# A fused conditioned block with an LSTM: a later reciprocal, an attention product and injections at other steps, and a scan that adds first

## What is computed

```
# L0: attention over two keys (a learned no-op and the condition), 16 heads
w = softmax(q @ k);  x = x + (w @ v) @ W_proj + b_proj
# L1: one shared SwiGLU expert, 8 routed gelu experts, top 2 by a sigmoid router
s = sigmoid(x @ router_w.T + t_bias)
topk of s + router_bias;  denom = sum of the 2 chosen s
gates = s_sel / (denom + EPS)  (1/2 where denom <= EPS)
x = x + (shared + sum of gates * expert) / 3
# L2: x = x + u @ W_u + x @ W_e,   u = gelu(cond @ W_proj + b_proj)
# L3: an LSTM over the 1024 tokens, 256 wide
z = x_t @ Wx + b + h @ Wh;  i, f, o = sigmoid(z_i), sigmoid(z_f), sigmoid(z_o);  g = tanh(z_g)
c = f * c + i * g;  h = o * tanh(c);  y_t = x_t + h
```

## Time and profile before

| | before |
|---|---|
| median of 3 runs | 2413.18 us (2410.02 to 2414.47) |
| the profiled execution | 2409.16 us |
| its span, first to last instruction | 2407.4 us |
| granted TensorE clock, share of full speed | 0.996 |
| PE busy, PEld busy | 2051.9 us (85%), 1505.9 us (63%) |
| DVE, POOL, ACT busy | 1420.3 us (59%), 1169.1 us (49%), 876.7 us (36%) |

### The profile page before, as it was taken

How to read it: one execution, slowest core, us unless ns; L and a number is a source line. 1 busy time by engine, 2 the same in 40 slices (tenths; PEclk the granted TensorE clock), 3 DMA queues, 4 the chain that set the end, 5 groups by cost and what they waited for, 6 DMA issues and landing times.

```text
span 2407.4 us, 200920 instructions
## 1 busy us (share of the span) xinstructions
PE 2051.9 (85%) x86306; PEld 1505.9 (63%) x86306; DVE 1420.3 (59%) x7602; ACT 876.7 (36%) x4761; POOL 1169.1 (49%) x5082
## 2 busy tenths in 40 slices
PE   6888888888888888888888888888888888888888
PEld 4666666666666666666666666666666666666666
DVE  2565665566566556656655665665566566556655
ACT  1333333333333333333333333333333333333333
POOL 3445445444544554454455445445544544544454
PEclk8999999999999999999999999999999999999999
DMA  3000000000000000000000000000000000000000
GB/s 135 4 3 2 3 3 2 2 3 3 2 3 3 2 2 3 3 2 3 3 2 2 3 3 2 3 3 2 2 3 3 2 3 3 2 2 3 3 2 3
DMA packets 57581, 14.54 MB, mean 6 GB/s; under 512 B 56161, under 2 KB 56161, under 8 KB 57058
## 3 DMA queue, kind: packets, MB, share of 16 engines
q1 hardware_dynamic: 57570, 14.39, 2.6%
HBM read 12.26 MB, written 2.10 MB: 6 GB/s over the span
## 4 chain that ended last, share of the span: by engine, by line
PE 37%; POOL 22%; DVE 20%; issue 12%; ACT 9%; DVEq 0%; POOLq 0%; ACTq 0%
PE bank L885 28%; DVE bank L678 9%; ACT terms L513 5%; DVE bank L686 5%; PE bank L792 5%; DVE h_ring L702 4%; ACT bank L519 4%; PE bank L742 3%; POOL beats L386 2%; POOL ties L387 2%; POOL ties L389 2%; POOL beats L391 2%; POOL lead L384 2%; POOL beats L358 1%; POOL top L394 1%
## 5 line engine op out<-in xcount | busy, mean ns | idle before, releaser
L885 PEld LDWEIGHTS bank<-wh_sb,h_ring 128*4 128x4 f32 (+2 forms) x65536 | 922.9, 94 | 705.9 <-DVE h_ring L702 700.1
L885 PE MATMUL bank<-wh_sb,h_ring 128*4 128x64 f32 (+2 forms) x65536 | 1107.9, 219 | 296.8 <-DVE h_ring L702 229.7
L510 ACT ACTIVATE f_act<-bank 128x4 f32<-128x4 f32 x1024 | 177.3, 173 | 1026.0 <-DVE bank L676 1026.0
L676 DVE STREAM_TRANSPOSE bank<-bank 128x64 f32<-128x64 f32 x1024 | 271.6, 265 | 390.7 <-PE bank L885 390.7
L678 DVE STREAM_TRANSPOSE bank<-bank 128x64 f32<-128x64 f32 x1024 | 271.5, 265 | 186.1 <-PE bank L885 186.1
L513 ACT ACTIVATE terms<-bank 128x8 f32<-128x8 f32 x1024 | 189.5, 185 | 280.3 <-DVE bank L678 280.3
L372 POOL TENSOR_TENSOR num<-one,fall 128x8 f32<-128x8 f32 x130 | 26.0, 200 | 532.1 <-ACT fall L467 532.1
L754 PE MATMUL bank<-up_sb,x 128*32 128x512 f32 x2080 | 274.0, 599 | 0.7 <-ACT fall L467 0.7
L684 DVE STREAM_TRANSPOSE bank<-bank 128x64 f32<-128x64 f32 x1024 | 271.6, 265 | 0.1
L760 PE MATMUL bank<-down_e,hid_t 128*16 128x256 f32 x3096 | 266.6, 380 | 0.0
L702 DVE SCALAR_TENSOR_TENSOR h_ring<-o_act,bank 128x4 f32<-128x4 f32 x1024 | 161.0, 157 | 138.6 <-ACT bank L519 95.0
(11 more groups left out here) (133 smaller groups left out, 2654.2 us busy)
## 6 DMA issues: line engine op xcount, KB each, us to landing
x_a<-in_x SPq DMA_DIRECT2D x129, 16.0 KB, 1.7
x_s<-in_x SPq DMA_DIRECT2D x129, 16.0 KB, 1.7
up_sb<-in_up SPq DMA_DIRECT2D x1, 2048.0 KB, 8.7
out_y<-y_sb SPq DMA_DIRECT2D x128, 16.0 KB, 1.4
down_sb<-in_down SPq DMA_DIRECT2D x1, 1536.0 KB, 12.5
wx_sb<-in_wx SPq DMA_DIRECT2D x1, 1024.0 KB, 14.2
wh_sb<-in_wh SPq DMA_DIRECT2D x1, 1024.0 KB, 16.3
wkv_sb<-in_wkv SPq DMA_DIRECT2D x1, 512.0 KB, 3.9
```

The lines of the kernel that those rows point to most:

```text
L510: nc.scalar.activation(f_act[:, :].rearrange("p (c b) -> p c b", b=B), t_f_b[:, :, fo:fo + B], ACT.Tanh).then_inc(a_f, 1)
L676: nc.vector.transpose(bank[3][:, 0:HC], z_f_b[:, 0:HC]).then_inc(t_f, 1)
L885: last = nc.tensor.matmul(z[32 * j:32 * j + row + B, 0:HC], h_ring[:, prev, c, WIN - B - row:WIN], wh_v[:, c, g, j, :], start=False, stop= ...
```

## The change

Four things are changed, and a few waits with them.

1. **Late reciprocal.** `invert_inv` goes from the end of u = 5 to the start of u = 7 on DVE, behind `hidden_s`. `turn(0, hid_s)` goes from the start of u = 0 to the end of u = 7.
2. **Attention's product.** `attend` goes from the end of u = 7 to u = 3, behind `sum_mm`, into another bank (7 in place of 5). x3_made is now signalled behind it, and stream_made behind the last down product of u = 0 instead of behind the layer 2 product.
3. **Injections.** g and i are injected at u = 6, f and o at u = 7; `GI_AT = 6` now shifts the rows of g and i. `pad` copies the shifted window and stands inside `gates`, behind the subtraction `lead`.
4. **Scan.** The cell's scan is state = (addend + state) x factor. Per cell the four pairs are factor 0 (clears the state), tanh of i, tanh of g, 0.5, and addend 1, 1, 1, kept part. The factors lie in PSUM (bank 4), where ACT writes them; the addends lie in SBUF.

The diff, cut:

```
-FO_AT = 6
+GI_AT = 6
...
-        terms = sb("terms", [P, 2 + 8 * NCELL])
-        factor = terms[:, 0:4 * NCELL]
-        addend = terms[:, 1 + 4 * NCELL:1 + 8 * NCELL]
-        gi_out = terms[:, 2:2 + 8 * NCELL].rearrange("p (g q k) -> p g q k", g=2, k=4)[:, :, :, 0]
-        keep_out = addend.rearrange("p (q k) -> p q k", k=4)[:, :, 2]
+        addend = sb("addend", [P, 4 * NCELL])
+        keep_out = addend[:, :].rearrange("p (q k) -> p q k", k=4)[:, :, 3]
...
+        factor = bank[4][:, HC:HC + 4 * NCELL]
+        factor_q = factor.rearrange("p (q k) -> p q k", k=4)
+        gi_out = factor_q[:, :, 1:3].rearrange("p q h -> p h q")
...
-        attn_b = bank[5][:, 64:64 + C * NB].rearrange("p (c t) -> p c t", c=C)
+        attn_b = bank[7][:, D + C * NB:D + 2 * C * NB].rearrange("p (c t) -> p c t", c=C)
...  (POOL)
-                return pool.tensor_copy(padded[:, :, NB:2 * NB], x3[:, :, NB:2 * NB])
+                return pool.tensor_copy(padded[:, :, NB:2 * NB], x3[:, :, BEHIND:BEHIND + NB])
...
                 pool.tensor_tensor(lead[:, :, :], rivals, own_sel, ALU.subtract).then_inc(gate_step, 1)
+                if between:
+                    between()
...
-                gates(i * U + (READY + U))
-                pad(i * U + (READY + U)).then_inc(padded_out, U)
+                gates(i * U + (READY + U), lambda: pad(i * U + (READY + U)).then_inc(padded_out, U))
...  (DVE, main loop)
-                    if u == 0:
-                        dve.wait_ge(hid_s_out, now)
-                        turn(0, hid_s[:, :], hid_st, U)
...
                     elif u == 7:
-                        hidden_s(now, U)
+                        hidden_s(now)
+                        invert_inv(now)
...
-                    nc.vector.tensor_tensor_scan(cell_all, factor, addend, 0.0, ALU.mult, ALU.add).then_inc(cell, 1)
+                    nc.vector.tensor_tensor_scan(cell_all, addend[:, :], factor, 0.0, ALU.add, ALU.mult).then_inc(cell, 1)
...
-                    elif u == 5:
-                        invert_inv(now)
                     elif u == 6:
                         hidden_a(now)
+                    elif u == 7:
+                        dve.wait_ge(hid_s_out, now)
+                        turn(0, hid_s[:, :], hid_st, U)
...  (PE, main loop)
                     if u == 0:
                         pe.wait_ge(hid_st, now)
-                        stream_mm(U)
+                        stream_mm()
                         cond_mm()
-                        down_mm(0)
+                        down_mm(0).then_inc(stream_made, U)
...
                     elif u == 3:
                         pe.wait_ge(partial_out, now)
-                        sum_mm(U)
+                        sum_mm()
+                        pe.wait_ge(own_out, now)
+
+                        attend(attn_b).then_inc(x3_made, U)
...
                     elif u == 6:
-                        pe.wait_ge(t_f, now)
-                        inject_fo(z_f_b, GF)
-                        pe.wait_ge(t_o, now)
-                        inject_fo(z_o_b, GO)
-                    elif u == 7:
                         pe.wait_ge(padded_out, now)
                         pe.wait_ge(t_gi, now)
                         inject_gi()
-                        pe.wait_ge(own_out, now)
-                        attend()
+                    elif u == 7:
+                        pe.wait_ge(t_f, now)
+                        inject_fo(z_f_b, GF)
+                        pe.wait_ge(t_o, now)
+                        inject_fo(z_o_b, GO)
```

More of the change, by code:

```diff
@@ L362, in add_eight, with gates @@
                 pool.tensor_tensor(out, terms[:, :, 0:1], terms[:, :, 1:2], ALU.add).then_inc(gate_step, 1)
-            def gates(count):
+            def gates(count, between=None):
                 rivals = sel[:, :].unsqueeze(1).to_broadcast([P, E, E])
@@ L621, in _ @@
             hidden_a(U)
-            hidden_s(U, U)
+            hidden_s(U)
             dve.wait_ge(hid_s_out, U)
@@ L738, in scores, with attend @@
                     nc.tensor.matmul(scores_b, score_w[:, c, :], x_s[:, c, :], start=(c == 0), stop=(c == C - 1))
-            def attend():
+            def attend(attn):
                 for c in range(C):
-                    last = nc.tensor.matmul(attn_b[:, c, :], value_w[:, c * P:(c + 1) * P], w1_own[:, :],
+                    last = nc.tensor.matmul(attn[:, c, :], value_w[:, c * P:(c + 1) * P], w1_own[:, :],
                                             start=True, stop=True)
@@ L761, in tile_mm, with stream_mm @@
                                         skip_group_check=True)
-            def stream_mm(up_to):
+            def stream_mm():
                 for c in range(C):
                     last = tile_mm(c, x1[:, c, 0, 0:NB], we_sb[:, c, :], True)
-                last.then_inc(stream_made, up_to)
+                return last
             def cond_mm():
@@ L831, in _ @@
             pe.wait_ge(we_ident, C)
-            stream_mm(READY)
+            stream_mm().then_inc(stream_made, READY)
             pe.wait_ge(w_in["wproj2"], 16)
@@ L924, in _ @@
                     elif u == 6:
+                        pe.wait_ge(padded_out, now)
+                        pe.wait_ge(t_gi, now)
+                        inject_gi()
+                    elif u == 7:
                         pe.wait_ge(t_f, now)
@@ L928, in _ @@
                         inject_fo(z_o_b, GO)
-                    elif u == 7:
-                        pe.wait_ge(padded_out, now)
-                        pe.wait_ge(t_gi, now)
-                        inject_gi()
-                        pe.wait_ge(own_out, now)
-                        attend()
 _INS = ("x", "small", "wkv", "wq", "wproj", "up", "we", "down", "wproj2", "wu", "wx", "wh", "bias_z")
```

73 lines of the change are left out of this document (37 added, 36 removed).

## The result

The changed kernel takes 2179.12 us (median of 4 runs, 2177.69 to 2179.5) against 2412.98 us before: ratio 0.9031, 95% interval 0.9015 to 0.9047. It is 234 us faster. The direction and the sizes of the two large terms were right; two of the small terms were not, and one of the two large ones was put down to one move where two were needed.

A forecast was written before the change was run, and what follows sets the result against it. The prediction took the recurrence chain to bound the kernel, with steps 5, 7 and 0 longer. Savings of 1.54 us per batch plus 0.06 from the scan, times 128, made 205 us: 2205, plus 4, gave 2209, range 2192 to 2240.

The forecast's parts named there:

- the two large terms: Late reciprocal: step 5 from 3.09 to 2.08 us. Attention and injections moved: step 7 from 2.68 to 2.08 us.
- The reciprocal's stall: DVE's wait for den_eps at step 5: moving the reciprocal to step 7 removes 1.01 us per batch.
- The attention product: PE: step 7 loses 0.52 us of loads; behind the sum at step 3 they cost 0.01 us.
- B: PE at step 3: attention costs what it cost at step 7, up to 0.52 us per batch: 2276 us; chance 0.04.
- C: POOL's late gates move the stall to h_read in step 0, 0.6 us per batch: 2286 us; chance 0.03.
- the scan: ACT's tanh 15 ns less into PSUM, DVE's scan 5 ns more: net 10 ns less in six steps, 0.06 us per batch.
- A: DVE's scan is dearer in PSUM, net 35 ns more in seven steps: 2248 us, 2262 by the page; chance 0.07.
- D: Slower than before: addition first makes the scan's elements 16 ns dearer, net 0.24 us per step: 2463 us; chance 0.01.
- PE's account of steps 3 and 6: PE, not the chain, sets both: step 3 becomes 2.09 us (attention loads), step 6 2.14 (injection of g and i).
- the 4 us at the end: Added to 2205 us because the median of the runs lay 4 us above the profiled execution: 2209.
- the injections: PE: with g and i, step 6 becomes 2.14 us, not 2.08; with f and o, step 7 becomes 2.08.
- the early pad: On POOL, pad ahead of den_eps makes that sum 0.2 us later, 5.0 us after step 4's start; nothing waits.

The follow-up runs named there:

- part 2 alone: The kernel before with only the attention product moved to step 3, in bank 7, with its signals: 2355.3 us, ratio 0.9769.

## Why the prediction was wrong

**Right.** The two places that bound a batch beside the chain, and their prices. The reciprocal's stall of 1.01 us per batch, 129 us forecast, is 125 in the run with reciprocal and pad; den_eps ends 5.07 after the start of step 4 (5.0 forecast), hid_e 2.75 after the start of step 7 (2.8), half_h 2.95 (3.1). The attention product fits at step 3 behind the sum: with part 2 alone step 3 still lasts 2.08. In the change the stalls did not reappear anywhere (rivals B and C), and the scan was not dearer (A and D).

**Mis-sized: the scan.** "The net is 10 ns less per step, in the six steps" was 28 ns, and not in six steps only. Two terms were off. ACT's eight values gained 23 ns and not the 15 that four values gave: the range had 15 as its end, taken from another shape. And the scan with one operand in PSUM took 5 ns less, where I had 5 more and a range of 0 to 24 from pairs of adds. Undone in the changed kernel (its placement alone), this part costs 31 us; the prediction had 8. This is the larger part of the miss: with the 28 ns in all eight steps the forecast would have been some 21 us lower. The rule of 120 cycles against 58 in the Trainium skill ("VectorE: DVE Perf Modes", TRN2 errata) did not show itself in the scan, which took 196 ns with an operand in PSUM and 199 without. The Trainium skill also says ("ScalarE: Activation LUTs", the note on ScE to PSUM) that ScalarE is faster into PSUM than into SBUF. The trace agrees, with 162 ns against 185, and this was the larger effect.

**Wrong: PE's account of steps 3 and 6.** "The load behind it started at 2.14. So step 6 becomes 2.14" took the start of a 128-column load for the time at which PE is free. The run with the product at step 7 shows 0.11 us in front of such a load and 0.02 in front of a narrow one. In the change the injections' loads end 2.04 after the start of step 6, h is there at 2.00, and the step lasts 2.06. With the factors back in SBUF step 6 lasts 2.09 and step 3 2.08, where this account has 2.14 and 2.09. At step 3 the wide loads of sum and attention overlap (the second group starts 0.44 after the first, not 0.53), so step 3 is the chain's. This account held up to 0.07 us per batch too much (0.01 and 0.06), 9 us, and it also kept these two steps from gaining by the scan. That leaves about 0.14 of the 0.21 to the scan, 18 us.

**Wrong: the 4 us at the end.** The sum came to 2205 for the profiled execution, and I added 4 because the profiled execution of before lay 4 below its median. That was the scatter of one execution: the profiled one of the change took 2179.15, its median. So of the 30 us between 2209 and 2179, 27 are in the batches and the other 3 come from this.

**Right by luck: the injections.** I held their exchange for neutral. It is worth 23 us, since with the old order PE's loop turns too late once the attention product has left step 7. Before, that product stood between the two, and the turn did not show: the recurrence started 0.02 after the last attention load. The 0.60 of step 7 (77 us) thus took two parts to remove: attention's move gives 56 us, the exchange 23 more. I had put all of it down to the first, so the total for step 7 came out right by luck.

**Not seen: the early pad.** I counted it as a cost of 0.2 us on POOL. It is the condition of the largest gain: 2417 without it, 2286 with it.

**Not seen: the order of the waits in step 0.** I held its extra 0.06 for given. It was in reach of an exchange of two lines, 11 us.

The parts add up: 125 + 56 + 23 + 31 = 235 us of 234. The first two were done alone on the kernel before and the last two undone in the change; the parts act on one another (the scan is worth 18 us alone and 31 in the change), so another choice of runs gives another sum.

## What to carry to other kernels

In a chain with stalls, a gain per step counts only in steps that the chain itself sets: the shorter tanh and scan were worth 18 us before the stalls were gone and 31 after. When something is moved later, list what stands behind it in the same queue, and move those first that somebody waits for; and look for what an engine's loop branch stands behind. A size that was measured in one shape (four values per partition) need not hold in another (eight): measure the very shape, above all where its cost counts in every step.

## What the runs showed of the hardware

- Two semaphore waits ahead of one DVE instruction: with the one that is satisfied late as the last, step 0 lasts 2.12 us, with the one that is long satisfied as the last, 2.05.
- The turn of PE's loop: behind an injection of 24 matmuls the next weight load started 0.20 and 0.21 us after the last one had ended, and 0.01 after where the branch had been moved elsewhere. It cost 0.16 us per batch with part 2 alone and 0.18 in the changed kernel, and showed nothing behind the attention product (0.02 to 0.03).
- TensorE's loop of 8 steps ran with 8 packets of instruction DMA in all; of 32 steps with 705 packets (11.55 MB), and the kernel took 541 us more in the one case (2743 against 2202) and 445 in the other (2800 against 2355), at a mean granted clock of 0.955 and 0.948.
- A 128-column weight load started 0.11 us after the last of the injections' narrow loads had ended, a narrow one 0.01 to 0.02 us after; behind four score loads of 32 columns the 128-column load started after 0.03.
- ACT's tanh of eight values per partition took 185 ns into SBUF and 162 into PSUM; of four values 173 and 158.
- DVE's scan of 16 elements took 199 ns with both operands in SBUF and 196 with one in PSUM (medians).
- All three reciprocals of the router stand on DVE, and POOL's rows show none; whether POOL could take one no run tried.
